# First-layer expert weights read from memory tile by tile in the fourth feed-forward stage

## What is computed

```
logits = (x @ wg_red.T) @ wg_unit.T
gates = softmax(logits); expert = argmax(gates); score = max(gates)
for e in range(8):
    h = gelu(x @ w1[e] + b1[e])            # 128 -> 512
    out += (expert == e) * (h @ w2[e] + b2[e])   # 512 -> 128
out = out * score
```

## Time and profile before

| | |
|---|---|
| time before, median of 3 runs | 6176.57 us (6176.3 to 6177.36) |
| the profiled execution, its own time | 6192.15 us |
| its span | 6190.4 us |
| PE busy | 92% of the span |
| POOL busy | 47% |
| DMA engines busy, last two of 40 slices | 0.2 and 0.3, at 90 and 98 GB/s |
| the feed-forward stage of the fourth block | from 6014 us of the span to its end |

### The profile page before, as it was taken

How to read it: one execution, slowest core, us unless ns; L and a number is a source line. 1 busy time by engine, 2 the same in 40 slices (tenths; PEclk the granted TensorE clock), 3 DMA queues, 4 the chain that set the end, 5 groups by cost and what they waited for, 6 DMA issues and landing times. The chain is left out here.

```text
span 6190.4 us, 102241 instructions
## 1 busy us (share of the span) xinstructions
PE 5696.1 (92%) x33833; PEld 3015.6 (49%) x33833; DVE 4316.9 (70%) x9755; ACT 3846.1 (62%) x8213; POOL 2913.7 (47%) x2774
## 2 busy tenths in 40 slices
PE   8999999689997999999999889999999999987758
PEld 3444444422222666666666634444444444455448
DVE  4555554178785777777877678888888888775545
ACT  2444444256665777777777667777777777754336
POOL 1224326456766766666666432233233233233448
PEclk9999999799998999999999999999999999998989
DMA  2001001221111111111111110000000000023123
GB/s 47 15 15 40 24 16 45 73 62 35 33 33 32 40 34 32 32 32 39 45 43 42 36 30 13 15 15 13 16 14 12 18 13 13 9 66 98 40 90 98
DMA packets 304270, 219.34 MB, mean 35 GB/s; under 512 B 27890, under 2 KB 279668, under 8 KB 303492
## 3 DMA queue, kind: packets, MB, share of 16 engines
q1 hardware_dynamic: 284578, 177.38, 11.1%
q0 software_dynamic: 12544, 29.71, 1.4%
q10 hardware_dynamic: 6626, 5.72, 0.3%
HBM read 97.11 MB, written 73.87 MB: 28 GB/s over the span
## 5 line engine op out<-in xcount | busy, mean ns | idle before, releaser
L3861 PE MATMUL a_scores_ps<-a_kT,a_q_mixed 128*128 128x512 f32 x2048 | 1046.4, 593 | 3.2 <-ACT a_probs L3671 3.1
L3871 PE MATMUL a_acc_ps<-a_probsT,a_v_post 128*128 128x512 f32 x2048 | 1042.8, 592 | 0.4 <-DVE a_probsT L3764 0.4
L3671 ACT ACTIVATE a_probs<-a_scores_ps,a_neg_max 128x512 f32<-128x512 f32 x1024 | 702.4, 686 | 429.7 <-DVE a_neg_max L3754 420.3
L3754 DVE TENSOR_REDUCE a_neg_max<-a_scores_ps 128x1 f32<-128x512 f32 x1024 | 693.3, 677 | 202.1 <-PE a_scores_ps L3861 197.3
L3764 DVE STREAM_TRANSPOSE a_probsT<-a_probs 128x512 f32<-128x512 f32 x1024 | 715.5, 699 | 135.8 <-PE a_acc_ps L3871 112.5
L3676 ACT ACTIVATE a_probs<-a_probs,a_inv_sum 128x512 f32<-128x512 f32 x1024 | 727.6, 711 | 0.8 <-DVE a_inv_sum L3759 0.8
L3042 DVE TENSOR_REDUCE a_neg_max<-a_pair_ps 128x2 f32<-128x1024 f32 (+3 forms) x512 | 417.6, 824 | 354.7 <-PE a_pair_ps L3138 348.2
L2847 ACT ACTIVATE a_probsT<-a_pair_ps 128x1024 f32<-128x1024 f32 (+3 forms) x512 | 359.0, 703 | 485.0 <-PE a_pair_ps L3151 468.1
L3871 PEld LDWEIGHTS a_acc_ps<-a_probsT,a_v_post 128*128 128x128 f32 x2048 | 389.0, 190 | 490.9 <-issue 488.8
L3861 PEld LDWEIGHTS a_scores_ps<-a_kT,a_q_mixed 128*128 128x128 f32 x2048 | 384.4, 190 | 476.0 <-issue 438.5
L3617 POOL TENSOR_TENSOR a_q_mixed<-a_qT,a_pre 128x512 f32<-128x512 f32 x248 | 250.0, 1040 | 758.7 <-PE a_scores_ps L3861 758.7
(11 more groups left out here) (420 smaller groups left out, 11866.8 us busy)
## 6 DMA issues: line engine op xcount, KB each, us to landing
f_v_even<-f_v_odd SPq DMA_DIRECT2D x224, 130.0 KB, 2.3
a_v<-a_v_rows SPq DMA_DIRECT2D x256, 64.0 KB
f_x_tiles<-routed_x SPq DMA_DIRECT2D x72, 193.0 KB
attention_out<-a_s_out SPq DMA_DIRECT2D x48, 256.0 KB, 2.3
routes_y_rows<-a_zeros SPq DMA_DIRECT2D x32, 256.0 KB
a_parts<-routes_y_rows SPq DMA_DIRECT2D x32, 256.0 KB, 3.6
f_x<-x_after SPq DMA_DIRECT2D x32, 256.0 KB
f_gx<-x_after SPq DMA_DIRECT2D x32, 256.0 KB, 3.2
```

What stands on the lines that cost most here:

```text
L3671: act.activation(probs[:, n % NPR, :], scores_ps[n % NS][:], ACT.Exp, bias=neg_max[:, n % NS:n % NS + 1], scale=1.0, accum_out=row_sum[:, ...
L3754: dve.tensor_reduce(neg_max[:, n % NS:n % NS + 1], scores_ps[n % NS][:], AX.X, ALU.max, negate=True).then_inc(max_ready, 1)
L3861: pe.matmul(scores_ps[n % NS][:], q_mixed[:, g % 2, i].rearrange("f a q -> f (a q)"), kT[:, par, :], start=True, stop=True).then_inc(score ...
L3871: pe.matmul(acc_ps[par][:], v_post[:, g, i, :], probsT[:, g % NT, i, :], start=(p == 0), stop=(p == U - 1)).then_inc(products_done, 1)
```

## The change

The full first-layer table is no longer held on chip, and its 2 MB load at the start of the attention phase goes. `w1_now` becomes a ring of 8 buffers. SP fills it: for each tile it reads the expert's place from the table `at_i` into a register and issues a DMA of 128 rows of 2048 bytes, 256 KB, from device memory. POOL's copies go; POOL keeps the scatters, now without the lag. SP's order is: the four row loads of the first group each followed by a weight load, the weight loads of tiles 4 to 7, the row loads of groups 1 to 4, and then for each tile i from 8 on a row load (of group i // 4 + 3, as long as there are any) and the weight load of tile i. The PE waits on the DMA's semaphore where it waited on the copy's.

```diff
-        self.w1, self.w2 = sb("w1", [D, E * I]), sb("w2", [P, E * I])
+        self.w2 = sb("w2", [P, E * I])
+        self.w1 = dram["L3f_w1"].rearrange("d n i -> d (n i)")
...
-        self.loads = [(self.w1[:], dram["L3f_w1"].rearrange("d n i -> d (n i)")),
-                      (self.w2[:], dram["L3f_w2"].rearrange("i n d -> i (n d)")),
+        self.loads = [(self.w2[:], dram["L3f_w2"].rearrange("i n d -> i (n d)")),
...
-    SCATTER_LAG = 11
-    RING, W_RING = 6, 4
+    RING, W_RING = 6, 8
...
         def _(sp):
-            for g in range(GROUPS):
-                if g >= RING:
+            def load_tile(g, t):
+                i = g * GROUP + t
+                if t == 0 and g >= RING:
                     sp.wait_ge(y_kept, g - RING + 1)
                     sp.wait_ge(homes_ready, g - RING + 1)
+                at = sp.value_load(at_row[0:1, i:i + 1], min_val=0, max_val=E * routed_rows.SEGMENT - P)
+                sp.dma_start(x_tiles[:, g % RING, t, :], routed_rows.x[bass.ds(at, P), :]
+                             ).then_inc(tiles_loaded[g % RING], 16)
+
+            def load_w1(i):
+                if i >= W_RING:
+                    sp.wait_ge(hidden_done, i - W_RING + 1)
+                e = sp.value_load(at_i[0:1, i:i + 1], min_val=0, max_val=(E - 1) * I)
+                sp.dma_start(w1_now[:, i % W_RING], w1[:, bass.ds(e, I)]).then_inc(w1_loaded[i % W_RING], 16)
+
+            for t in range(GROUP):
+                load_tile(0, t)
+                load_w1(t)
+            for i in range(GROUP, W_RING):
+                load_w1(i)
+            for g in range(1, RING - 1):
                 for t in range(GROUP):
-                    i = g * GROUP + t
-                    at = sp.value_load(at_row[0:1, i:i + 1], min_val=0, max_val=E * routed_rows.SEGMENT - P)
-                    sp.dma_start(x_tiles[:, g % RING, t, :], routed_rows.x[bass.ds(at, P), :]
-                                 ).then_inc(tiles_loaded[g % RING], 16)
+                    load_tile(g, t)
+            for i in range(W_RING, TILES):
+                g = i // GROUP + RING - 1 - W_RING // GROUP
+                if g < GROUPS:
+                    load_tile(g, i % GROUP)
+                load_w1(i)
...
-            def pick_w1(i):
-                e = pool.value_load(at_i[0:1, i:i + 1], min_val=0, max_val=(E - 1) * I)
-                if i >= W_RING:
-                    pool.wait_ge(hidden_done, i - W_RING + 1)
-                pool.tensor_copy(w1_now[:, i % W_RING], w1[:, bass.ds(e, I)]).then_inc(w1_picked, 1)
...
-            for i in range(TILES + SCATTER_LAG):
-                if i < TILES:
-                    pick_w1(i)
-                if i >= SCATTER_LAG:
-                    scatter_tile(i - SCATTER_LAG)
+            for i in range(TILES):
+                scatter_tile(i)
...
             def up(i):
                 pe.wait_ge(tile_kept, i + 1)
-                pe.wait_ge(w1_picked, i + 1)
+                pe.wait_ge(w1_loaded[i % W_RING], 16 * (i // W_RING + 1))
```

More of the change, by code:

```diff
@@ L1479, in routed_experts_phase @@
         tiles_loaded = [sem(f"tiles_loaded{n}") for n in range(RING)]
-        tile_turned, tile_kept, w1_picked = sem("tile_turned"), sem("tile_kept"), sem("w1_picked")
+        tile_turned, tile_kept = sem("tile_turned"), sem("tile_kept")
+        w1_loaded = [sem(f"w1_loaded{n}") for n in range(W_RING)]
         hidden_done, hidden_ready = sem("hidden_done"), sem("hidden_ready")
@@ L1490, in _ @@
         def _(sp):
-            for g in range(GROUPS):
-                if g >= RING:
+            def load_tile(g, t):
+                i = g * GROUP + t
+                if t == 0 and g >= RING:
                     sp.wait_ge(y_kept, g - RING + 1)
                     sp.wait_ge(homes_ready, g - RING + 1)
-                for t in range(GROUP):
-                    i = g * GROUP + t
-                    at = sp.value_load(at_row[0:1, i:i + 1], min_val=0, max_val=E * routed_rows.SEGMENT - P)
-                    sp.dma_start(x_tiles[:, g % RING, t, :], routed_rows.x[bass.ds(at, P), :]
-                                 ).then_inc(tiles_loaded[g % RING], 16)
+                at = sp.value_load(at_row[0:1, i:i + 1], min_val=0, max_val=E * routed_rows.SEGMENT - P)
[12 more added lines that the diff above has]
+            for g in range(1, RING - 1):
+                for t in range(GROUP):
+                    load_tile(g, t)
[4 more added lines that the diff above has]
+                load_w1(i)
+            for g in range(TILES // GROUP + RING - 1 - W_RING // GROUP, GROUPS):
+                for t in range(GROUP):
+                    load_tile(g, t)
             for n in range(4):
```

## The result

The changed kernel takes 6204.65 us (median of 5 runs, 6203.61 to 6206.37), the kernel before 6177.36 us beside it (5 runs, 6176.30 to 6186.03). The ratio is 1.0041 with an interval of 1.0027 to 1.0056: slower by 27 us. Predicted were 6203.3 us, in a range of 6189 to 6222.

The account below looks back on a forecast made before the run. SP's issuing was to become the bound: 22.0 and 128.8 us of intervals, 2 of waits, 2.59 of landing and 22.8 of last tiles put the last `up` 26.7 us later; 6176.6 + 26.7 = 6203.3 us, range 6189 to 6222.

Parts of the forecast that it names:

- SP becomes the bound: Stage from 6014 us: SP's two loads per tile take 2.32 us, longer than PE's 1.90 and POOL's 2.06.
- the third rival: SP's wait on DVE or half-clock PE feeds back: up to 10 or 20 us, 6213 to 6223; 0.15 with second rival.
- The interval: SP's time per table-addressed load: 1.10 us for the first 20 intervals, 1.16 for the other 111.
- The 2 us taken for the passed waits: SP's weight loads from tile 8 on: semaphore waits normally long reached, between nothing and 5 us, taken as 2.
- The register read: SP's table read into a register: measured 268 ns used, not the skill's 600 ns, which would add some 43 us.
- The rival "not slower": Transfers (1.95 us) or PE (1.90) set the pace: 6170 to 6174 us; 0.15 together with intervals near 1.0 outside the profile.
- Landing and last tiles: Stage's end: tile 59's weights land 2.59 us after issue, then 12 PE steps of 1.90, 22.8 us, to the last `up`.
- The hole before tile 8: PE stands some 7 us, near 6042 to 6049, hidden in SP's chain; the lower clock may return for a few tiles.
- The tail: From the last `up` to the kernel's end: 24.6 us, hanging on DVE, taken as unchanged.
- The sum: Stage's SP chain, landing and last tiles put the last `up` at 6192.5 against 6165.8: 26.7 us later.
- The clause on the 15.6 us: Fourth rival: profiled execution exceeded the median by 15.6 us; if SP's reads are part, some of the 26.7 us go.
- POOL's busy time: Sign in the profile after: POOL busy about 72 us less.

Follow-up runs that it names:

- paced counterpart: Kernel before without copies, every tile using the first expert's weights, each scatter also waiting for the first-layer matmuls of 10 more tiles: 6168.16 us, ratio 0.9977.

## Why the prediction was right, point by point

**SP becomes the bound.** Right. Row and weight loads come at 1.09 us in the undisturbed stretches, SP waits for 2.3 us in all, and PE's turns follow the landings; taking 8 loads or the register reads away moves the last `up` by about what the theory asks for the loads (7.5 us for 8), and by most of it for the reads (19.3 us, where at least 24 were forecast). SP's waits, which the third rival feared to cost up to 10 or 20 us, are the 2.3.

**The interval.** The first 20 intervals were summed at 22.0 us and took 21.7; the other 111 at 1.16 each, 128.8 us, took 129.4, so 1.166 each with the waits in them. Tile 59's weights were issued after 151.1 us; the sum had 152.8. The 2 us taken for the passed waits were too much: the interval ahead of a weight load, which has one, is 1.09 us, and that ahead of a row load the same. A wait that is already met costs SP nothing that can be read here.

**The register read.** The Trainium skill (DMA: Bandwidth & Descriptors, "Latency and other measured facts") has a floor of about 600 ns for it. The added reads have a median of 272 ns, and the sum by the rows came out within 1.2 us at the last `up`; by that floor the sum would have been some 44 us late.

**The rival "not slower".** Rejected. SP needs 2.3 us for a pair of loads whose bytes need less, an estimated 1.95 by the prediction. The windows after the change put it lower still: 227 GB/s at a share of 0.77 are 295 at a share of 1, so 525 KB take 1.78 us, an estimate too. The sentence of the Trainium skill (DMA: Bandwidth & Descriptors, "Issuing engines are not separate DMA queues") that the time to start a DMA is usually small beside the DMA itself is borne out by the trace for one load, 1.09 us against a landing of 3.1. For the stream of loads it is not: there the issues take longer than the bytes.

**Landing and last tiles.** The landing was taken as 2.59 us, from the quiet start of the stage; with the DMA share at 0.77 it is 3.1. Twelve steps of 1.90 us followed. The last `up` is at 177.0 us where the sum had 178.2: 1.7 us early at the issue (151.1 for 152.8), 0.6 back from there to tile 59's `up` (3.2 us for 2.6).

**The hole before tile 8.** It exists, smaller than said: the turn of tile 9 and that of tile 10 are 6.47 us apart instead of 1.90, so PE lost 4.6 us. It stood for 2.95 of them, not 7, and as predicted the clock fell behind the halt: the granted clock was 0.50, the lower level of 1.2 GHz, from 6037 to 6039 us, and that `up` took 2.05 us instead of 1.06. SP's chain hid it: tile 9's `up` is 4.2 us behind its weights' issue, and by tile 15 the lag is down to 3.2.

**The tail.** Taken as unchanged at 24.6 us, it is 22.4. The 2.2 us were not DVE's: in the second profile of the kernel before the tail is 23.2 us, and in all others without late signals 22.3 to 22.4; the 0.9 us between these were not followed up. The first profile has late signals in it, of 1.2 and 2.7 us, at the last tiles, and DVE stood 3.4 us for one of them. So this term was mis-sized in the main because it came from one execution.

**The sum.** 178.2 + 24.6 = 202.8 us of stage predicted, 199.4 measured; before, 176.1 and 175.5. The loss in the stage is 23.3 to 23.9 us, the sum said 26.7, and the medians differ by 27.3 with an interval of 17 to 35 us. The near hit of the median is thus better than the working deserves: two or three us of it are chance. The place of the stage's start alone varies between 5993.8 and 6007.3 us among profiles without late signals.

**The clause on the 15.6 us.** The prediction feared that SP's reads are slower in a profile. They are not the reason; most of the excess lay 4800 us before the stage. And the changed kernel's profiled execution, 6203.61 us, was the shortest of its five, so taking the profile did not lengthen it.

**POOL's busy time.** "About 72 us less" was a slip: 72 copies of 0.91 us are 66, and it fell by 57.5. Nothing in the sum hangs on it.

## What to carry to other kernels

Before moving work from a compute engine to DMA, multiply the number of issues by the whole interval of the issuing queue (read, arithmetic, issue, taken from a stretch where it waits for nothing) and compare this with the pace of the stage; 1.1 us for a table-addressed load is more than half a tile here. Where a copy engine is a little over the pace and an issuing queue has room, move only as much as brings both down to it: here one tile in four by SP was worth 11 us where all of them cost 27. Don't take a term from one profile if a second one of the same kernel can be had.

## What was not expected of the hardware

In some sessions TensorE's signals reach the other engines up to 3.5 us after the start of the last matmul (0.29 us otherwise, 0.49 at most), several at a time, once for each run of four scatters by POOL, while TensorE's own records go on. It put the last `up` of the stage without any copy or load 28 to 29 us later than in its paced counterpart, which had no late signals (173.5 and 172.8 against 144.5). It was seen on two chips, and one of these showed none in another session. What the condition is, and whether spacing the scatters avoids it, stays open; the first profile of the kernel before speaks for the spacing, and the changed kernel itself was not measured in it.

SP's issue of one load usually takes 0.33 us but 0.45 to 1.6 us now and then, in 5 of 144 loads at a mean of 227 GB/s and in 20 of 144 at 254 GB/s. What makes it longer is not shown.
